# Grouped attention of a fused two-layer network: head and output weights held once in single precision, one product per tile in place of a high and a low one

## The reference

```python
def _div_clamp_fp8(x, scale):
    y = jnp.clip(x.astype(jnp.float32) / scale, -FP8_MAX, FP8_MAX)
    y = y.astype(jnp.bfloat16).astype(jnp.float32)
    return _fp8_roundtrip(y)

def _fp8_linear_pertensor(x, wq, w_scale, in_scale):
    xq = _div_clamp_fp8(x, in_scale)
    return jnp.einsum('bsi,oi->bso', xq * in_scale, wq) * w_scale

q  = _ln(_fp8_linear_pertensor(ln_out, wq, wq_scale, q_in_scale).reshape(b, s, g, hpg, d), ...)
k  = _ln(_fp8_linear_pertensor(ln_out, wk, ...).reshape(b, s, g, d), ...)
v  = _fp8_linear_pertensor(ln_out, wv, ...).reshape(b, s, g, d)
core = _gqa(q, k, v).reshape(b, s, nh * d)
qx = _ln(_fp8_linear_pertensor(ln_out, wqx, ...), ...)
kx, vx = jnp.split(jnp.einsum('bsi,oi->bso', cond, w_kv_x), 2, axis=-1)   # kx through _ln as well
xout = _gqa(qx, kx, vx).reshape(b, s, nh * d)
catq = _div_clamp_fp8(jnp.concatenate([core, xout], axis=-1), proj_smooth)
return jnp.einsum('bsi,oi->bso', catq, wproj) * (proj_in_scale * proj_w_scale)
```

## Time and profile before

| | |
|---|---|
| median of 3 runs | 928.32 us (925.02 to 929.63) |
| the profiled execution | 930.36 us |
| its span from first to last instruction | 927.8 us |
| mean granted clock of TensorE | 0.984 of full |
| TensorE busy | 867.2 us, 93% of the span |
| VectorE busy | 705.5 us, 76% |
| ScalarE busy | 563.2 us, 61% |

### The profile page before, as it was taken

The page is one execution under the profiler, slowest core; times in us unless marked ns, Lnnn a source line. Parts: engine busy times, 40 slices in busy tenths (PEclk is TensorE's granted clock), DMA queues, the critical chain, the costliest instruction groups (busy, mean ns, idle before and its releaser), DMA issues.

```text
span 927.8 us, 15314 instructions
## 1 busy us (share of the span) xinstructions
PE 867.2 (93%) x4998; PEld 646.8 (70%) x4998; DVE 705.5 (76%) x1557; ACT 563.2 (61%) x2045; POOL 133.6 (14%) x186
## 2 busy tenths in 40 slices
PE   5999999999988888999999999999999999899997
PEld 3657666666656766878888787878788787655554
DVE  3682553665688788888879988888888888897853
ACT  3541324565574875867878787787778687751411
POOL 3000030200001322111212122121212121100000
PEclk9998999999999998999999999999999999999999
DMA  7001000000010123333243242333332235421000
GB/s 234 1 0 57 1 0 1 2 2 1 24 36 24 58 68 80 81 94 78 68 112 100 70 123 73 73 101 77 94 83 78 64 75 160 110 70 25 1 23 23
DMA packets 63952, 56.76 MB, mean 61 GB/s; under 512 B 11073, under 2 KB 62850, under 8 KB 63874
## 3 DMA queue, kind: packets, MB, share of 16 engines
q1 hardware_dynamic: 63776, 55.76, 22.2%
q10 hardware_dynamic: 98, 0.03, 0.0%
HBM read 21.15 MB, written 1.05 MB: 24 GB/s over the span
## 4 chain that ended last, share of the span: by engine, by line
PE 69%; DVE 16%; SPq 6%; issue 4%; ACT 3%; DMA 2%; POOL 1%; DVEq 0%; ACTq 0%
PE ps L950 11%; PE ps L963 9%; PE ps L892 7%; SPq L589 6%; PE ps L978 5%; PE ps L1036 4%; PE ps L917 4%; PE ps L937 3%; PE ps L744 3%; PE ps L734 2%; PE ps L757 2%; PE ps L722 2%; PE ps L831 2%; PE ps L796 2%; PE ps L855 2%
## 5 line engine op out<-in xcount | busy, mean ns | idle before, releaser
L1361 ACT ACTIVATE group_probs<-ps,score_bias 128x256 f32<-128x256 f32 x256 | 117.2, 483 | 51.0 <-DVE score_bias L1786 51.0
L1786 DVE TENSOR_REDUCE score_bias<-ps 128x2 f32<-128x512 f32 x128 | 87.3, 690 | 41.9 <-PE ps L963 41.6
L963 PE MATMUL ps<-group_kT,group_qT 128*128 128x256 f32 x512 | 116.5, 381 | 0.3 <-ACT group_qT L1327 0.3
L963 PEld LDWEIGHTS ps<-group_kT,group_qT 128*128 128x128 f32 x512 | 97.7, 191 | 26.8 <-issue 7.8
L1303 ACT ACTIVATE group_squares<-ps 128x128 f32<-128x128 f32 x384 | 105.3, 346 | 8.7 <-PE ps L892 8.3
L1303 ACT ACTIVATION_READ_ACCUMULATOR group_squares<-ps 128x1 f32 x384 | 97.7, 280 | 0.0
L1349 ACT ACTIVATE group_cat_y<-ps,vec_inv 128x256 bf16<-128x256 f32 x128 | 53.6, 470 | 60.5 <-PE ps L950 57.5
L2133 POOL TENSOR_TENSOR head_rstd<-head_sum,minus_half 128x7 f32<-128x7 f32 (+1 forms) x64 | 86.6, 1353 | 5.3
L892 PE MATMUL ps<-group_w_hi,front_xq 128*128 128x256 f32 x256 | 74.1, 317 | 0.0
L2132 POOL TENSOR_SCALAR head_sum<-head_sum 128x7 f32<-128x7 f32 (+1 forms) x64 | 13.6, 213 | 413.7 <-ACT group_values_x L1318 413.6
L1797 DVE TENSOR_SCALAR group_probs<-group_probs,score_inv 128x256 f32<-128x256 f32 x256 | 72.7, 347 | 0.2
(11 more groups left out here) (296 smaller groups left out, 1977.0 us busy)
## 6 DMA issues: line engine op xcount, KB each, us to landing
second<-laid SPq DMA_DIRECT2D x256, 64.0 KB, 2.1
group_probsT<-front_quant SPq DMA_DIRECT2D x240, 64.0 KB, 2.1
group_raw_p<-in_L_xattn_wproj_dram SPq DMA_DIRECT2D x16, 256.0 KB, 3.3
group_raw_w<-in_L_xattn_wq_dram SPq DMA_DIRECT2D x8, 256.0 KB, 2.9
group_raw_w<-in_L_xattn_wqx_dram SPq DMA_DIRECT2D x8, 256.0 KB, 3.1
group_raw_w<-in_L_xattn_w_kv_x_dram SPq DMA_DIRECT2D x16, 128.0 KB, 3.2
x_all<-in_x_dram SPq DMA_DIRECT2D x2, 512.0 KB, 6.2
front_work<-in_ctx_dram SPq DMA_DIRECT2D x1, 1024.0 KB, 7.0
```

The source lines that it names most:

```text
L963: last = pe.matmul(c.ps[:, bank, t * S:(t + 1) * S], c.qT[:, side, h, t * P:(t + 1) * P], c.kT[:, side, :], start=True, stop=True)
L1361: last = act.activation(c.probs[:, side, h, t, :], c.ps[:, fills.bank(name), t * S:(t + 1) * S], ACT.Exp, bias=c.score_bias[:, i:i + 1], a ...
L1786: v.tensor_reduce(c.score_bias[:, i:i + 2], c.ps[:, bank, :].rearrange("p (t n) -> p t n", n=S), AX.X, ALU.max, negate=True).then_inc(nega ...
```

## The change

- `w_hi`/`w_lo`, `kv_hi`/`kv_lo` and `wp_hi`/`wp_lo` become `w`, `kv_w` and `w_p`, one float32 tile each. `xq` and `cat` become float32. Placeholder tiles keep the other addresses where they were.
- Each product is one float32 matmul in place of two float32r matmuls.
- ScalarE's write of the weight is now the last reader of the bank and drains it. VectorE's `take_weight` and `next_weights` are gone, and with them `hi_ready`, `HI_ORDER` and `splits_early`.
- `turns_early` now holds for all slots from 4 on that are not led by an even group, also those in which weights are turned. This moves L937 ahead of L978 in nine more slots (6, 7, 12, 13, 14, 20, 21, 22, 26).

```diff
-        self.turns_early = n >= 4 and not led and all(w == 4 for _, w in self.weights)
-        self.splits_early = n >= 4 and not led and not self.turns_early
-        self.adds_early = n >= 4 and not led
+        self.turns_early = self.adds_early = n >= 4 and not led
...
         def head_weights(w, g):
 
             pair = w in PAIR_FILLS
-            hi, lo = (c.kv_hi, c.kv_lo) if pair else (c.w_hi[g % 2], c.w_lo[g % 2])
             at = w % 2 * W_WIDTH
-            return hi, lo, slice(at, at + W_WIDTH)
+            return (c.kv_w if pair else c.w[g % 2])[:, :, at:at + W_WIDTH]
...
                         for k in range(KD):
                             x_ = c.xq[:, b // 2, kind, k, b % 2 * S + t * P:b % 2 * S + (t + 1) * P]
-                            for m, w in enumerate((hi, lo)):
-                                last = pe.matmul(c.ps[:, bank, at:at + W_WIDTH], x_, w[:, k, cols],
-                                                 start=k == 0 and m == 0, stop=k == KD - 1 and m == 1)
+                            last = pe.matmul(c.ps[:, bank, at:at + W_WIDTH], x_, w[:, k, :], start=k == 0, stop=k == KD - 1)
...
                         for i in range(4):
-                            for m, w in enumerate((c.wp_hi[par], c.wp_lo[par])):
-                                last = pe.matmul(c.ps[:, bank, t * D:(t + 1) * D], c.cat[:, i, t * P:(t + 1) * P],
-                                                 w[:, i, :], start=i == 0 and m == 0, stop=i == 3 and m == 1)
+                            last = pe.matmul(c.ps[:, bank, t * D:(t + 1) * D], c.cat[:, i, t * P:(t + 1) * P],
+                                             c.w_p[par][:, i, :], start=i == 0, stop=i == 3)
...
-                            last = act.activation(hi[:, k, cols], c.ps[:, bank, k * W_WIDTH:(k + 1) * W_WIDTH],
+                            last = act.activation(scaled[:, k, :], c.ps[:, bank, k * W_WIDTH:(k + 1) * W_WIDTH],
                                                   ACT.Copy, scale=c.w_scale[:, w, k:k + 1])
-                        last.then_inc(hi_ready, 1)
+                        fills.drain(last, name)
...
-                def take_weight(name, w, g):
...
-                    v.wait_ge(hi_ready, HI_ORDER.index((g, w)) + 1)
...
-                            last = v.scalar_tensor_tensor(out=lo[:, k, cols], in0=c.ps[:, bank, k * W_WIDTH:(k + 1) * W_WIDTH],
-                                                          scalar=c.w_scale[:, w, k:k + 1], in1=hi[:, k, cols],
-                                                          op0=ALU.mult, op1=ALU.subtract)
...
-                    fills.drain(last, name)
...
         front = overlay("front", [
-            ("xq", F32R, 2, 4, KD, HALF),
+            ("xq", F32, 2, 4, KD, HALF),
```

More of the change, by code:

```diff
@@ L22 @@
 F32 = mybir.dt.float32
-F32R = mybir.dt.float32r
 BF16 = mybir.dt.bfloat16
@@ L196 @@
 W_PLAN.update({24: [(7, 0)], 25: [(7, 1), (7, 4)], 26: [(6, 6), (6, 7)], 28: [(7, 6)], 29: [(7, 7)]})
-HI_ORDER = [(0, w) for w in range(4)] + [at for n in sorted(W_PLAN) for at in W_PLAN[n] if at[1] != 4]
 def head_fills(g):
@@ L1290, in take_weight @@
                     else:
-                        act.activation(c.wp_hi[par][:, HPG * (w - 6):HPG * (w - 5), :],
-                                       c.ps[:, bank, :].rearrange("p (h n) -> p h n", h=HPG),
-                                       ACT.Copy, scale=c.out_scale[:]).then_inc(hi_ready, 1)
+                        ins = act.activation(c.w_p[par][:, HPG * (w - 6):HPG * (w - 5), :],
+                                             c.ps[:, bank, :].rearrange("p (h n) -> p h n", h=HPG),
+                                             ACT.Copy, scale=c.out_scale[:])
+                        fills.drain(ins, name)
                 def next_weights(o, which=slice(None)):
@@ L1736, in round_kind @@
                                     e.rearrange("p (k n) -> p k n", k=KD), ALU.subtract).then_inc(split_kind, 1)
-                def take_weight(name, w, g):
-                    if w == 4:
-                        return
-                    bank, par = fills.bank(name), g % 2
-                    v.wait_ge(hi_ready, HI_ORDER.index((g, w)) + 1)
-                    if w < 4:
-                        hi, lo, cols = head_weights(w, g)
-                        for k in range(KD):
-                            last = v.scalar_tensor_tensor(out=lo[:, k, cols], in0=c.ps[:, bank, k * W_WIDTH:(k + 1) * W_WIDTH],
-                                                          scalar=c.w_scale[:, w, k:k + 1], in1=hi[:, k, cols],
-                                                          op0=ALU.mult, op1=ALU.subtract)
-                    else:
-                        rows = (slice(None), slice(HPG * (w - 6), HPG * (w - 5)), slice(None))
-                        last = v.scalar_tensor_tensor(out=c.wp_lo[par][rows], in0=c.ps[:, bank, :].rearrange("p (h n) -> p h n", h=HPG),
-                                                      scalar=c.out_scale[:], in1=c.wp_hi[par][rows], op0=ALU.mult, op1=ALU.subtract)
-                    fills.drain(last, name)
-                def next_weights(o, which=slice(None)):
-                    for g, w in o.weights[which]:
-                        take_weight(("W", g, w), w, g)
                 def normalise_item(o, tiles=(0, 1)):
@@ L1838, in visit @@
                         invert_sums(o, 1)
-                    if o.weights and o.n >= 4 and not o.splits_early:
-                        next_weights(o)
                     if o.outputs and o.adds_early:
@@ L2030, in _ @@
                         normalise("C", 1, x[1], xn[1], normed[1])
-                    for w in FIRST_STEPS.get(i, ()):
-                        take_weight(("W", 0, w), w, 0)
                 for i in (STEPS - 3, STEPS - 1):
@@ L2268, in build @@
             ("under_xq", F32, 16, 512),
[L2269 to L2271 removed]
+            ("w0", F32, KD, 512), ("under_kv", F32, KD, 512), ("kv_w", F32, KD, 512), ("under_w_x0", F32, KD, 512),
+            ("w_x0", F32, KD, 2 * P), ("w_p0", F32, 4, D), ("under_w_p1", F32, 4, D),
+            ("w_p1", F32, 4, D), ("under_keys", F32, 4, D), ("keys_b", F32, B, 2, HD), ("w1", F32, KD, 512),
             ("heads", F32, 2, 2, 6, HD), ("raw_w", F32, 6, D), ("raw_kv", F32, 4, D), ("raw_p", F32, 2, 2, HPG * HD),
[L2273 removed]
+            ("qT", F32, 2, HPG, S), ("kT", F32, 2, S), ("cat", F32, 4, S), ("cat_y", BF16, 4 * S), ("cat_e", BF16, 4 * S),
             ("values_x", F32, 4, 2, HD), ("probsT0", F32, 2, BLOCKS, 2 * P), ("squares", F32, 2, 7, HD),
[L2275 removed]
+            ("values", F32, B, 2, 2, HD), ("under_w_x1", F32, KD, 512), ("w_x1", F32, KD, 2 * P),
             ("probs", F32, 2, HPG, 2, S)])
[L2277 to L2280 removed]
+        c.kv_w, c.raw_kv, c.keys_b, c.values_x = (group[n] for n in ("kv_w", "raw_kv", "keys_b", "values_x"))
+        c.w, c.w_x, c.w_p = ([group[f"{n}{par}"] for par in range(2)] for n in ("w", "w_x", "w_p"))
         c.squares, c.heads, c.raw_w, c.raw_p, c.cat = (group[n] for n in ("squares", "heads", "raw_w", "raw_p", "cat"))
```

20 lines of the change are left out of this document (3 added, 17 removed).

## The result

The kernel after took 1027.16 us, the median of 4 runs (1026.25 to 1029.51); beside them the kernel before had 927.93 (4 runs). The ratio is 1.1054, 95% interval 1.1026 to 1.1083: a tenth slower. The forecast was 1030.3, its range 1017 to 1042. The profiled execution after took 1027.18 us, its span is 1025.4, so the two spans differ by 97.6 us against the 102.0 of the sum. One run of e11 (926.89 us) and two of the kernel before (1261.93 and 1467.75) fell in a slower state of the chip, and all medians and ratios here are of the other runs.

What follows compares the result with a forecast made beforehand. TensorE was taken to bound slots 5 to 31: +103.2 there, -5.0 of waits, -0.8 in slots 0 to 4 and +4.6 in slots 32 to 35 make +102.0 us, on 928.3 giving 1030.3 us, range 1017 to 1042.

Steps and rivals of the forecast that it cites:

- What bounds the kernel: Slots 5 to 31: TensorE, busy 426.61 of 433.49 us, sets the time; VectorE's spared work is worth nothing by itself.
- The price of a product: Each of 640 products goes from 0.239 to 0.431 us, +0.1925; in slots 5 to 31, 536 products, +103.2 us.
- the rival of 0.170 a product: The tail hides in the new blocks too: +0.170 us a product, about 1018 us; chance 0.09.
- one record: Rival: a product costs one record, as little as a float32r matmul, 0.119 us; about 895 us; chance 0.02.
- The 5.0 us of waits: Slots 5 to 31: longer slots take back all of TensorE's waits, -5.0 us, bounds 0 to -6.9.
- The move of the turning: Nine slots: turning the heads ahead of the output products adds no wait, 0 us, with 2.5 us of cover.
- The low parts ahead of the stage: Attention stage: four low parts of the first weights, 1.49 us, leave the chain, -1.5 us.
- Slots 0 to 4 and the clock in slot 4: Pipeline fill: -0.8 us with the first low parts, between -3 and +7; slot 4's output products at full clock, no change.
- the forecast's other value: Slot 4: output products again at 1.2 GHz, making the sum 3.4 us higher.
- Slots 32 to 35: Pipeline drain, 32 products: +1.5 in slot 32, 0 in 33, +3.1 in 34 and 35; +4.6 us, between +3 and +6.2.
- The move makes a wait: Rival: in the nine slots and before short ones, VectorE's layout and SP end behind TensorE; about 1050 us; chance 0.06.
- VectorE sets the pace: Rival, slots 5 to 31: TensorE only looks full, VectorE's low parts, about 24 us, come off; 987 us; chance 0.05.

Runs made afterwards that it cites:

- e11: e5 with the scaled write of the head weights moved from ScalarE to VectorE, low part still left out: 915.65 us, ratio 0.9865.
- e2: Kernel before without VectorE's low parts; each low product reads the high part again, so the low part is left out: 924.87 us, ratio 0.9946.
- e3: Kernel before with one float32 product for the head weights alone; output weights keep high and low part: 984.37 us, ratio 1.0595.
- e4: Kernel before with one float32 product for the output weights alone; head weights keep high and low part: 969.03 us, ratio 1.0435.
- e5: Kernel after with its products' operands rounded to float32r, one high product each, the low part left out: 910.48 us, ratio 0.9784.
- e1: Kernel after with the turning of the heads back at its old place in the nine slots: 1029.44 us, ratio 1.1097.
- e8: Kernel after with the heads turned ahead of the output products in all slots from 4 on, leading ones too: 1024.7 us, ratio 1.1020.
- e6: Kernel before with the heads turned ahead of the output products in the nine more slots, low parts and products unchanged: 932.12 us, ratio 1.0028.
- e7: Kernel after with slot 31 alone turned back, output products ahead of the turning: 1025.59 us, ratio 1.1036.
- e10: e5 with the turning back at the place of the kernel before in the nine slots, low part still left out: 910.56 us, ratio 0.9764.

## Why the prediction was right

**What bounds the kernel.** Right. e2 took 20 us off VectorE and gained 3 in the stage; e3, e4 and the change made TensorE's products dearer and paid for each.

**The price of a product.** Right, and it is nearly the whole result. Forecast +0.1925 us each; leading slots give 4.59 / 24 = 0.191, and L970 takes 3.46 us for 16 records in the chain, 0.216 each. (The chain before also has 16 records of L892 in 1.91 us, at 601.57, which the earlier trace rows doesn't show.) The tail under the next block stayed exposed: the rival of 0.170 a product would have made a leading slot 20.99 us, and it was 21.50. That a product would have one record is out by the 512 records above, and e5 shows what it would have been worth. The rule cited from the Trainium skill, "FP8 and Floating Point Precision", section TensorE Precision Notes, four passes for FP32, gave an estimated 0.427; the chain shows 0.431 to 0.433.

**The 5.0 us of waits.** Right: no wait of TensorE is left in slots 5 to 31. e3 and e4 show that a change four to six tenths this size takes them back as well, all but 0.4 us. But 1.2 us of them came up again in slot 32, behind the stage; see there.

**The move of the turning, costed at nothing.** The one step of the stage that was mis-sized, by -3.0 us: I asked only whether the move adds a wait (it doesn't, the 2.5 us of cover held) and not whether the blocks run differently behind other neighbours. 3.67 us for L950 was a row of the chain, and I read it as the price of the averages; it is their price behind the turning. With e1's order the stage is 530.45 us, against the 531.7 of the forecast. The remaining 1.2 us is the difference between 0.1925 and 0.191 over 536 products (0.8), and rounding. The slot that took 15.2 us (slot 12) takes 17.7 and not the 18.3 of the forecast: 0.33 us by the move, the rest because L978 took 2.15 us there before, not 1.91.

**The low parts ahead of the stage.** -1.5 forecast. The stretch ahead of the second half of slot 0 lost 3.2 us (the first half's 8 products cost nothing, as forecast: from the first of them it is 9.88 us before and 9.89 after), which leaves them 0.7: the other 2.5 stand there before any changed instruction has run. They are a net of clock: the execution after was ahead by 0.7 us at 53 us, by 4.0 at 115 (the start of the same block of L734, then L729, is at 115.56 before and 111.55 after), and by 2.5 at 176. 60 to 115 us, before and then after:

```profile
60.00:115.00 55.00, 51.56 (x196) 35.03 (x194) 28.41 (x60) 18.11 (x34) 2.76 (x4) 0.94 0.08 24
```

```profile
60.00:115.00 55.00, 50.99 (x203) 33.68 (x201) 30.31 (x69) 19.07 (x35) 3.96 (x6) 1.00 0.08 25
```

The granted clock is 0.94 in the one and 1.00 in the other: part of this stretch ran at 1.2 GHz before, all of it at 2.4 after. Of the experiments' traces some have the dip (e3, e8) and some not (e1, e2, e4), whatever their code, so it belongs to the execution and not to the change.

**Slots 0 to 4 and the clock in slot 4.** Right. +0.3 for +0.7, and slot 4 had the granted clock 1.00 where the earlier trace rows had 0.85. L970 of slot 4, behind its wait:

```profile
355.35 3.72 PE L970 MATMUL ps<-group_w_p,group_cat 128*128 128x256 f32 x16 [1.22 <-DVE group_cat L115]
```

The same products in e4, where the wait for the rounded inputs is still there:

```profile
353.62 5.36 PE L977 MATMUL ps<-group_wp_hi,group_cat 128*128 128x256 f32 x16 [2.04 <-DVE group_cat L116]
```

After the change 16 records take nearly the time in which the earlier trace rows had 16 cheaper ones at half the clock, 3.72 for 3.4 us: 1.8 times the work at twice the clock. The wait ahead fell from 2.04 to 1.22 us, and the wait for the rounded inputs (2.14) is gone. e4 is the case of the forecast's other value: it kept the waits of 2.12 and 2.04 us, its slot 4 had the granted clock 0.93, the first records of L977 step by 0.43 us and the last by 0.22, and the block takes 5.36 us. Over all traces it goes with the waits: before, e2, e4 and e6 have both of them and 0.85 to 0.93; after, e1, e7 and e8 have one of 1.2 to 1.3 us and e3 none, and their slot 4 has 1.00; e5, e10 and e11 have longer ones and 0.77 to 0.84. No run changed the waits and nothing else, so that they are the cause is borne out, not isolated.

**Slots 32 to 35.** +6.5 for +4.6, the other mis-sized term, and the step that failed is slot 32. I added its 8 products to its length, +1.5; the slot went from 15.95 to 18.73, +2.8. TensorE at the seam of slots 31 and 32, before:

```profile
796.86 1.96 PE L950 MATMUL ps<-group_probsT,group_values 128*128 128x512 f32 x4 [2.11 <-DMA group_probsT<-front_quant]
...
803.82 1.04 PE L642 MATMUL ps<-ident,last_xn 128*128 128x128 f32 x8
```

And after:

```profile
895.84 1.09 PE L637 MATMUL ps<-ident,last_xn 128*128 128x128 f32 x8 [0.71 <-DVE last_xn L1531]
...
900.80 0.63 PE L930 MATMUL ps<-ident,group_heads 128*128 128x128 f32 x4 [1.06 <-ACT group_probs L1354]
...
903.25 3.72 PE L970 MATMUL ps<-group_w_p,group_cat 128*128 128x256 f32 x16 [0.95 <-DVE group_cat L115]
```

From slot 32 on TensorE has no products of L886 to cover VectorE's chain. That chain begins in slot 31: L970 there ends at 888.25, and behind it stand VectorE's addition, layout, moments and normalisation (`last_xn`, to 895.78), which L637 waits for. Before, the same chain ended at 802.30, 1.5 us ahead of L642, because TensorE stood 2.11 us for a DMA in slot 31. The change took that wait back, and with it the time that had covered VectorE. So one of the waits that the sum counts as returned came up again as 0.71 us for `last_xn` and 0.3 us more for the probabilities (0.75 before, 1.06 after).

The move of L937 has no part in it: slot 31 turned early before as well, and in e1, with the old order, slot 32 is 18.73 us all the same. What slot 32 is longer than before, less 1.5 us where its products are the new ones, goes with the wait that is left in slot 31:

| run | DMA wait in slot 31 | slot 32 | more than its products |
|---|---|---|---|
| before | 2.11 | 15.95 | |
| e2, e6 | 2.02, 2.25 | 15.96, 15.95 | 0.0 |
| e4 | 0.40 | 18.10 | 0.6 |
| e3 | none | 16.94 | 1.0 |
| after, e1, e8 | none | 18.73, 18.73, 18.72 | 1.2 |
| e7 | none | 17.49 | 0.0 |

e7 ends L970 of slot 31 1.3 us earlier in its slot, and L638 (L637 of the kernel after) waits for nothing. So 1.2 of the missing 1.9 us are this wait. The rest, 0.6 us, stands behind the last output block of the trace after (72.51 us to the end; 71.92 in e1, e4 and e7), where its granted clock in the last 30 us was 0.97, against 0.98 in e7 and 0.99 in e1. Slots 33 to 35 cost the +3.1 of the forecast.

**The rivals.** None came true. "The move makes a wait" is out: no slot has a wait in the kernel after that e1 has not. "VectorE sets the pace" and "one record" were excluded by e2 and by the records. One sign missed its mark without touching the time: VectorE's busy time fell from 705.5 to 679.0 us, not to 671. The sum took count times mean, 34.4 us, where instructions that overlap count twice; the three groups were busy for 13.6 + 6.5 + 11.1 = 31.2 us. The other 4.7 us are open.

The errors cancel in part: -3.0 (neighbours), -0.8 (price), +1.9 (slot 32 and the last blocks), -0.4 (slots 0 to 4), -1.7 (ahead of the stage, most of it the clock) make -4.0 of the -4.4 us between the two spans.

## What to carry to other kernels

Count records and time them in the chain, by type, before believing "one in place of two": here one float32 product costs 0.431 us and two float32r products 0.239, so splitting an operand into a high and a low part is the cheap way, and VectorE's work for it was hidden. Where an engine is busy 98% of a stage, work taken from another is worth only what it gives back of the waits (3 us for 20 here), and the engine next in line may be closer than its busy share says: with 49 us less on TensorE the stage gained 10 to 15, since a loop through ScalarE of 16 us stood right behind. When blocks are moved, look at both seams. When a wait is counted as taken back, ask whose work ran under it, and look at the slot in which the pattern ends: there 1.2 of the 5.0 us came up again.

## What the runs showed of the hardware

- A block of 8 averages takes 3.43 to 3.45 us behind matmuls of 256 columns, of either type (after; before, slot 30), and 3.67, after a step of 0.09, behind 12 transposes, whatever type the projection ahead of these has (before, after and e1). Why is open; no run varied the transposes.
- In the chain, sixteen single-precision records take 3.45 us in a closed row of blocks, and 3.72 (L970, slots 4 and 32) behind a wait. From their start to the start of the next block it is 3.46 and 3.56 (slots 31 and 32), so 0.1 us is lost and the rest is a start that a closed row hides.
- Between about 60 and 115 us TensorE's granted clock fell to 0.94 in some executions and stayed at 1.00 in others with the same code up to there. e8 has the code of after up to slot 4 and reaches its first product of the groups' stage at 289.94 us, after at 284.79: spans of single traces can't be compared more finely than these 5 us without splitting off what lies ahead of the change.
